# Two of four scatter accumulators end four tiles earlier, and are read back one piece at a time

## What is computed

```python
scores = softmax(x @ gate_w.T);  topk_w, topk_ids = top_k(scores, 6)
comb = zeros(T, 64).at[arange(T)[:, None], topk_ids].add(topk_w / sum(topk_w))
gu = einsum('th,efh->tef', x, w_gate_up);  g, u = gu[..., :176], gu[..., 176:]
routed = einsum('tef,ehf->th', silu(g) * u * comb[:, :, None], w_down)
out = x + routed + shared            # shared: a dense gated layer over all rows
```

## Time and profile before

| what | us |
|---|---|
| median of 3 runs | 312.27 |
| lowest and highest run | 307.88, 314.04 |
| the profiled execution | 312.11 |
| its span, first to last instruction | 310.3 |

### The profile page before, as it was taken

The page is one execution under the profiler, slowest core; times in us unless marked ns, Lnnn a source line. Parts: engine busy times, 40 slices in busy tenths (PEclk is TensorE's granted clock), DMA queues, the critical chain, the costliest instruction groups (busy, mean ns, idle before and its releaser), DMA issues.

```text
span 310.3 us, 6611 instructions
## 1 busy us (share of the span) xinstructions
PE 266.9 (86%) x1698; PEld 231.7 (75%) x1698; DVE 144.0 (46%) x641; ACT 126.7 (41%) x376; POOL 184.5 (59%) x161
## 2 busy tenths in 40 slices
PE   7998767769786989999998999999999999999300
PEld 4595445557564768999988999999999999999200
DVE  3834887446675553543433333333333333344424
ACT  2515433222221254554444555555555555555200
POOL 8202277847586560867888676677666666665520
PEclk9999998958997999999999999999999999999955
DMA  6999999999332265899999999999999999959577
GB/s 171 385 420 427 415 363 392 393 393 348 112 143 108 95 138 179 247 318 336 355 344 361 318 329 331 324 328 325 326 331 339 331 331 330 222 57 266 111 174 268
DMA packets 48059, 89.07 MB, mean 287 GB/s; under 512 B 6604, under 2 KB 32285, under 8 KB 46997
## 3 DMA queue, kind: packets, MB, share of 16 engines
q1 hardware_dynamic: 26997, 63.58, 57.0%
q0 software_dynamic: 12816, 17.12, 26.3%
q10 hardware_dynamic: 8208, 7.94, 7.6%
HBM read 58.08 MB, written 30.54 MB: 286 GB/s over the span
## 4 chain that ended last, share of the span: by engine, by line
PE 68%; issue 8%; DMA 8%; DVE 7%; another core or an unknown queue 4%; ACT 2%; POOL 1%; SPq 0%; POOLq 0%; DVEq 0%; ACTq 0%
PE PS L1114 29%; PE PS L1126 9%; PE PS L1127 9%; DMA acc<-PT,IDR 5%; PE PS L982 5%; PE PS L1089 4%; PE PS L1103 3%; PE PS L939 2%; DMA CT<-in_ctxT 2%; PE PS L945 2%; PE PS L1057 1%; PE PS L952 1%; PE PS L960 1%; DMA CT<-acc 1%
## 5 line engine op out<-in xcount | busy, mean ns | idle before, releaser
L1114 PEld LDWEIGHTS PS<-XT,WA 128*128 128x128 f32 (+1 forms) x852 | 105.5, 187 | 4.2 <-issue 0.5
L1114 PE MATMUL PS<-XT,WA 128*128 128x128 f32 (+1 forms) x852 | 105.9, 274 | 0.3 <-issue 0.3
L469 POOL DMA_INDIRECT acc<-PT,IDR x51 | 80.0, 1568 | 37.0 <-ACT PT L628 14.5
L860 DVE TENSOR_TENSOR AC<-SG,PS 128x128 f32<-128x128 f32 x71 | 20.5, 288 | 101.1 <-ACT SG L602 78.7
L628 ACT ACTIVATE PT<-PS,WT 128x256 f32<-128x256 f32 x70 | 33.2, 474 | 31.6 <-issue 15.1
L423 POOL DMA_INDIRECT x_slots<-HX,SLOT x36 | 36.1, 1004 | 16.5 <-issue 9.7
L469 POOL DMA_INDIRECT out_rows<-PT,IDR x19 | 29.9, 1573 | 23.7 <-ACT PT L628 14.6
L1126 PE MATMUL PS<-WA,AC 128*128 128x256 f32 x140 | 42.1, 382 | 1.3 <-issue 1.3
L1127 PE MATMUL PS<-WB,AC 128*128 128x256 f32 x140 | 41.6, 379 | 0.0
L526 ACT COPY XT<-PS 128x256 f32<-128x256 f32 x73 | 27.0, 372 | 19.0 <-PE PS L982 10.9
L601 ACT ACTIVATE SG<-PS 128x128 f32<-128x128 f32 x71 | 19.7, 277 | 33.7 <-PE PS L1114 28.4
(11 more groups left out here) (143 smaller groups left out, 315.6 us busy)
## 6 DMA issues: line engine op xcount, KB each, us to landing
WA<-in_wa SPq DMA_DIRECT2D x71, 496.0 KB
x_slots<-WA SPq DMA_DIRECT2D x1, 8704.0 KB, 29.7
VXG<-x_slots ACTq DMA_DIRECT2D x57, 136.0 KB
WB<-in_wb SPq DMA_DIRECT2D x71, 48.0 KB
acc<-ZERO SPq DMA_DIRECT2D x2, 1152.0 KB
CT<-in_ctxT SPq DMA_DIRECT2D x2, 512.0 KB, 6.1
X<-in_x SPq DMA_DIRECT2D x2, 512.0 KB, 6.3
out_rows<-X SPq DMA_DIRECT2D x8, 128.0 KB
```

The source lines that it names most:

```text
L469: pool.indirect_dma_start(acc[j], bass.IndirectOffsetOnAxis(ap=IDR[:, u:u + 1], axis=0), YS[:, u % YR, :], None, compute_op=ALU.add).then_ ...
L860: v.tensor_tensor(AC[:, w % 2, 0, :], SG[:, w % 2, 0, :], PS[:, 4 + w % 2, 0:128], ALU.mult)
L1114: last = mm(PS[0:n, (4 if c == 2 else 2) + w % 2, c % 2 * 128:(c % 2 + 1) * 128], WA[:, base:base + n], XT[:, w % 2, k, :], start=(k == 0) ...
```

## The change

Two things.

1. A new constant `RETIRE = 60` takes the place of `E` (64) in `home`, `on_home` and `scattered`. Tiles 60 to 63 go to accumulators 0, 1, 0, 1 and not 0, 1, 2, 3. The last scatter of accumulator 2 is tile 58's, that of accumulator 3 tile 59's.
2. SP issues the four pieces of accumulators 2 and 3 one at a time: after each it waits until the piece has landed. The pieces of accumulators 0 and 1 are issued as before.

DVE's sums, the output writes, the weights' loads and the work of the tiles are unchanged.

```diff
+RETIRE = 60
         def home(t):
-            return t % NACC if t < E else t % 2
+            return t % NACC if t < RETIRE else t % 2
         def on_home(t):
-            return t // NACC if t < E else E // NACC + (t - E) // 2
+            return t // NACC if t < RETIRE else RETIRE // NACC + (t - RETIRE) // 2
         def scattered(eng, K, j):
             if j < 2:
-                eng.wait_ge(s_acc[j], (K + (1 - j + 2 * (E // NACC))) // 2 * 16)
+                eng.wait_ge(s_acc[j], (K + (1 - j + 2 * (RETIRE // NACC) + E - RETIRE)) // 2 * 16)
             else:
-                eng.wait_ge(s_acc[j], 16 * (E // NACC))
+                eng.wait_ge(s_acc[j], 16 * (RETIRE // NACC))
-            for j, landed in ((2, s_sum2), (3, s_sum3), (0, s_sum0), (1, s_sum1)):
+            for j, landed in ((2, s_sum2), (3, s_sum3)):
                 scattered(sp, K, j)
-                sums_in(sp, j, landed)
+                for c in range(MC):
+                    sum_in(sp, j, c, landed)
+                    sp.wait_ge(landed[c], 16)
+            for j, landed in ((0, s_sum0), (1, s_sum1)):
+                scattered(sp, K, j)
+                for c in range(MC):
+                    sum_in(sp, j, c, landed)
```

More of the change, by code:

```diff
@@ L231, in scattered, with sum_in @@
             if j < 2:
-                eng.wait_ge(s_acc[j], (K + (1 - j + 2 * (E // NACC))) // 2 * 16)
+                eng.wait_ge(s_acc[j], (K + (1 - j + 2 * (RETIRE // NACC) + E - RETIRE)) // 2 * 16)
             else:
-                eng.wait_ge(s_acc[j], 16 * (E // NACC))
-        def sums_in(eng, j, landed):
-            for c in range(MC):
-                eng.dma_start(SUM[j][:, c * MW:(c + 1) * MW], sums_of(j)[:, c * MW:(c + 1) * MW]).then_inc(landed[c], 16)
+                eng.wait_ge(s_acc[j], 16 * (RETIRE // NACC))
+        def sum_in(eng, j, c, landed):
+            eng.dma_start(SUM[j][:, c * MW:(c + 1) * MW], sums_of(j)[:, c * MW:(c + 1) * MW]).then_inc(landed[c], 16)
         def ge(eng, s, v):
```

## The result

The changed kernel takes 314.61 us (median of 22 runs, 309.64 to 319.76), the kernel before on the same chip 312.19 us (22 runs). The ratio is 1.008, with a 95% interval from 1.0044 to 1.0115: 0.8% slower, within 2%, where 0.5% faster was forecast. On two other chips, with shorter times for both kernels, it was 1.0108 (1.0071 to 1.0145) and 1.0088 (1.0056 to 1.0121). The measured 314.61 lies inside the range given. The side is the wrong one, and it is that of the second rival.

A forecast was written before the change was run, and what follows sets the result against it. Bound: scatters delayed by the burst of read-backs. 4.6 us won on the last scatter less 3.2 given back by late SP and crowded last read-backs: 312.1 - 1.4 = 310.7 us, range 306.2 to 315.1.

The forecast's parts named there:

- the second rival: SP's train of lone pieces becomes the bound and costs more than it gives; 4.3 us a piece gives 317.1 us; chance 0.25.
- What bounds the kernel: End of the chain: the burst reading accumulators 2 and 3 back makes tile 69's scatter start 5.0 us late.
- the first rival: SP is not late, scatters set the end: 8.93 us from tile 69's landing to the end, time 306.3; chance 0.25.
- The first lone piece: Start of SP's read-back of accumulators 2 and 3: first issue at 269.0, after tile 58's scatter lands in 4.1 us.
- the forecast gain of 1.4: Whole span: from 310.3 to 308.9 us, 4.6 won on the last scatter and 3.2 given back.
- A lone piece: SP's read-back of accumulators 2 and 3: 3.5 us for each piece waited for, 28.0 us for eight, SP free at 297.0.
- the break-even: SP's eight single pieces: at 3.68 us a piece, SP free at 298.45, the span equals that of before.
- The tail from X's issue: From accumulator 0's read-back at 297.0 to the end: 3.4 + 4.9 + 0.7 + 2.85 = 11.85 us.
- Scatters beside single pieces: Scatters on two accumulators, tiles 61 to 69: landing 4.3 us plus 0.83 to the next start; tile 69 starts at 292.5.
- the 4.6 us of gain: Tile 69's scatter: lands at 296.8 against 301.37 before, the gain from two accumulators and the burst going away.
- Structure: End of the chain: it goes through SP's pieces, X and CT issues back to back from about 297, DVE's sums before it.
- The likeliest case: The forecast's own case: SP free between 294.5 and 298.4, time 308.2 to 312.1 us; chance 0.40.

The follow-up runs named there:

- part 1 alone: Against the kernel before: accumulators 2 and 3 end with tile 59, their pieces still issued in bursts of four; ratios 1.0085, 1.0006 and 1.0015.
- part 2 alone: Against the kernel before: accumulators 2 and 3 still go on to tile 63, their pieces issued one at a time; ratio 1.0268, 316.86 us against 308.85.

## Why the prediction was wrong, point by point

**What bounds the kernel: right, and too hopeful.** That the burst beside the scatters makes tile 69's scatter late was right: two more profiles of before show the same 5.9 and 6.0 us behind ACT's last result, and with no reads it is 1.6 to 2.1. That the gain goes over to the end was not: with no reads at all the end is 17.1 to 17.6 us, about 3 below before, and from CT's issue to the end it takes 10.6 to 10.8 us and not the 8.9 of the first rival.

**The first lone piece: 269.0 forecast, 271.06 measured. This is the step that failed.** It took 4.1 us for tile 58's scatter, the landing of tile 63, and 0.4 more for remnants of weights: 4.6 us from the scatter's start at 264.43. But tile 63's scatter ran with the DMA engines half idle for the first part of its way, tile 58's with full ones. The stages showed it (share 1.09 up to 268), and a nearer row was tile 65's 7.88 us, also with full engines. Measured were 7.33, 7.47 and 7.43 us. That is 2.8 us more than the step had, of which 0.7 do not show in the 271.06, since this execution reached tile 58 0.7 us earlier (263.71). This term alone eats the forecast gain of 1.4. In part 1 alone, where nothing differs up to there, the same landing took 5.5, 6.6 and 7.2 us, so it is not a fixed number, and 4.1 is below all of them. In the changed kernel the stretch looks like this (columns as in the earlier trace rows):

```profile
262.00:268.00 6.00, 6.00 (x47) 5.75 (x46) 1.98 (x14) 3.04 (x9) 4.43 (x3) 1.00 1.10 337
268.00:272.00 4.00, 4.00 (x31) 3.79 (x31) 1.43 (x7) 2.09 (x7) 2.60 (x2) 1.00 1.01 221
```

**A lone piece: 3.5 us forecast, 3.69 measured** ((300.61 - 271.06) / 8, and 3.75 and 3.72 in the other profiles). The prediction had the break-even at 3.68, with a start of 269.0. A small miss, but it counts eight times: 1.5 us. That the price of a lone piece was the term to doubt, as the prediction said, holds; the start of the train cost more.

**The tail from X's issue: 11.85 forecast, 12.5 measured** (313.3 - 300.78; 12.7 and 12.8 in the others). In it CT's pieces queue behind X's: 5.43 us to landing on the chain, where the step added 0.70 us a piece. That is 0.7 us. Together: 308.9 + 2.1 + 1.5 + 0.2 (from the last landing to X's issue) + 0.7 = 313.4, against 313.3 measured. Counted from ACT's last result, which is the fairer sum, the forecast end was 308.9 - 290.15 = 18.7 us, and 18.7 + 2.8 + 1.5 + 0.2 + 0.7 = 23.9 is what was measured.

**Scatters beside single pieces: a cycle of 5.13 us forecast, 5.9 measured.** Tile 69's scatter started 4.6 us behind ACT's last result (4.3 and 5.3 in the other profiles), where 2.3 was forecast (292.5 - 290.15) and before had 5.9. It did not matter for the end, since SP's train was later still, but it was the ground on which the 4.6 us of gain stood. With the train shortened it came in part at best: 5.5 us with two in flight, 4.1 with pieces of 512 KB, and neither was faster than before.

**Structure: right.** That SP's train takes the place of the wait, that X's and CT's issues then follow back to back, that DVE's sums of 2 and 3 stay hidden, and where the change turns into a loss, all showed as told. The second rival had 0.25, and its sign held: X's issue came after 298.5. But its cause, a piece of 4.3 us, did not; the pieces cost 3.7, just at its break-even, and it was the late start that carried the train over. So that it named the side is in part luck, and so is that 314.61 lies inside the range. The likeliest case rested on three terms that all leaned the hopeful way, with a margin of only 0.18 us a piece.

## What to carry to other kernels

A read issued and waited for one at a time on an in-order queue is priced as count times round trip, and the round trip is that beside the other traffic; compute the break-even first, and if it lies within the error of the terms, forecast no side. Two in flight, or pieces twice as large, took the same bytes off the critical path, and the kernel was then as fast as before. And the landing time of a transfer is taken from a row with the same load on the DMA engines, not from the nearest in time: here 7.3 us for tile 58's scatter in the changed kernel, and 3.9 for tile 62's in the kernel before, which starts 10 us later.

## What was not expected of the hardware

A scatter of 128 rows lands in 3.7 to 3.9 us with the DMA engines half idle (tile 62's, in the seven profiles in which it releases the first read-back). Beside the weights it took 5.5 to 7.5 us (tile 58's, in eight profiles), about 8 (tile 56's, with the end at tile 55), and 9.23 in the row below, from the kernel with two in flight and the end at 59, 24 us before its first read-back. Beside the bursts of eight pieces the chains show 6.2 to 9.1.

```profile
246.26 9.23 DMA acc<-PT,IDR
```

What the scatters lose to the reads shows in when tile 69's starts behind ACT's last result. With nothing read beside it, and the end at tile 59 or 63, that is 1.6 to 2.1 us; with four lone pieces landed by then (part 2 alone) 3.0; with five or six of them (the change) 4.3 to 5.3; with all eight in bursts 5.3 to 7.1. So it rises with the bytes read beside the scatters, and how they are issued counts too: with the end at tile 63 the same eight pieces cost 5.9 to 6.0 in bursts and 3.8 and 4.9 with two in flight. These are one to three profiles each, and the end of the accumulators differs among them, so no run here separates the two shares.
